# Attention, output projection and an FP8-scaled product in one kernel: the first batch's last projection tiles move into the second batch's first groups

## What is computed

```python
q = (x @ wq_w.T + wq_b).reshape(b, t, H, HD)          # H = 32, HD = 32
k = (x @ wk_w.T + wk_b).reshape(b, t, HKV, HD)        # HKV = 1
v = (x @ wv_w.T + wv_b).reshape(b, t, HKV, HD)
scores = jnp.einsum('bqhd,bkd->bhqk', q, k1) / jnp.sqrt(jnp.float32(HD))
scores = jnp.where(causal, scores, -jnp.inf)
weights = jax.nn.softmax(scores, axis=-1)
attn = jnp.einsum('bhqk,bkd->bqhd', weights, v1).reshape(b, t, H * HD)
x = _layernorm(x + attn @ wo_w.T + wo_b)
x_sim = jnp.clip(x2 * x_scale, -448, 448)             # x_scale = 448 / max|x|, over all of x
w_sim = jnp.clip(weight * w_scale, -448, 448)         # w_scale = 448 / max|weight|
x = _layernorm(x + x_sim @ w_sim * (1.0 / (x_scale * w_scale)))
```

## Time and profile before

| | |
|---|---|
| median of 3 runs | 2719.75 us (2717.81 to 2719.91) |
| the profiled execution's own time | 2719.72 us |
| its span | 2718.0 us |
| mean granted TensorE clock | 0.974 |
| PE busy | 2542.1 us, 94% of the span |
| DVE busy | 1879.0 us, 69% |
| ACT busy | 1273.5 us, 47% |
| POOL busy | 865.6 us, 32% |

### The profile page before, as it was taken

One profiled execution on the slowest core, in us unless ns is written; L12 is line 12 of the kernel. 1 busy time (PEld: TensorE's weight loads), 2 busy tenths in 40 slices (PEclk: granted clock), 3 DMA queues, 4 the chain that ended last, 5 costly groups with the idle time before them and its releaser, 6 DMA issues.

```text
span 2718.0 us, 45333 instructions
## 1 busy us (share of the span) xinstructions
PE 2542.1 (94%) x15400; PEld 1588.6 (58%) x15400; DVE 1879.0 (69%) x1432; ACT 1273.5 (47%) x1571; POOL 865.6 (32%) x569
## 2 busy tenths in 40 slices
PE   7999998889999999999878999999999997799998
PEld 5888885545544444444544555444444445688887
DVE  6343336668788889999555788888899993444444
ACT  2222224545566666777334565666777670100000
POOL 2321302433322222212334333222221223566663
PEclk9999998989999999999888999999999998899999
DMA  7343334411211111011233122111101104122221
GB/s 232 124 145 141 116 128 141 122 40 51 62 45 39 39 40 40 12 39 40 67 95 94 44 66 51 40 39 39 40 29 37 39 1 162 48 85 90 88 93 62
DMA packets 75076, 197.24 MB, mean 73 GB/s; under 512 B 8559, under 2 KB 8559, under 8 KB 72815
## 3 DMA queue, kind: packets, MB, share of 16 engines
q1 hardware_dynamic: 50220, 140.52, 17.9%
q10 hardware_dynamic: 24768, 55.59, 5.3%
HBM read 123.72 MB, written 72.35 MB: 72 GB/s over the span
## 4 chain that ended last, share of the span: by engine, by line
PE 62%; issue 7%; DVE 5%; ACT 5%; POOL 3%; DMA 1%; ACTq 1%; SPq 0%; DVEq 0%; POOLq 0%
PE bank L1165 16%; PE bank L1177 15%; PE bank L1153 13%; PE bank L1261 13%; ACT prob L689 4%; DVE acc L940 3%; PE bank L1195 2%; POOL prob L546 2%; PE bank L1187 2%; DMA q_st<-max_d 1%; PE bank L1250 1%; DVE acc L937 1%; POOL att_lo L538 0%; ACT att_hi L700 0%; DVE r_den L901 0%
## 5 line engine op out<-in xcount | busy, mean ns | idle before, releaser
L689 ACT ACTIVATE prob<-bank 128x1024 f32<-128x1024 f32 (+3 forms) x1280 | 1077.4, 897 | 627.6 <-PE bank L1165 595.2
L940 DVE TENSOR_TENSOR acc<-acc,prob 128x2048 f32<-128x2048 f32 (+3 forms) x512 | 1093.4, 2136 | 131.1 <-POOL prob L546 85.8
L1165 PE MATMUL bank<-q_st,keys 98*128 98x512 f32 (+3 forms) x2560 | 712.5, 392 | 88.6 <-ACT prob L689 63.0
L1165 PEld LDWEIGHTS bank<-q_st,keys 98*128 98x128 f32 x2560 | 427.6, 192 | 391.6 <-ACT prob L689 308.3
L1177 PE MATMUL bank<-prob,v_t 128*32 128x512 f32 (+3 forms) x5120 | 596.6, 548 | 11.1 <-POOL prob L546 11.1
L546 POOL TENSOR_SCALAR_AFFINE_SELECT prob<-prob 128x512 f32<-128x512 f32 x256 | 300.8, 1179 | 873.0 <-ACT prob L689 872.4
L1075 PE MATMUL bank<-xt_hi,w_hi 128*128 128x512 f32 x576 | 227.3, 395 | 16.4 <-DVE xt_lo L777 15.7
L1075 PE MATMUL bank<-xt_hi,w_lo 128*128 128x512 f32 x576 | 226.6, 393 | 0.0
L1075 PE MATMUL bank<-xt_lo,w_hi 128*128 128x512 f32 x576 | 226.2, 393 | 0.0
L1177 PEld LDWEIGHTS bank<-prob,v_t 128*32 128x32 f32 x5120 | 107.9, 109 | 197.8 <-issue 141.4
L1261 PE MATMUL bank<-wf_hi,xs_hi 128*128 128x512 f32 x512 | 202.8, 396 | 0.0
(11 more groups left out here) (118 smaller groups left out, 2668.7 us busy)
## 6 DMA issues: line engine op xcount, KB each, us to landing
q_st<-q_hi_d SPq DMA_DIRECT2D x128, 256.0 KB
xt_raw<-x_t SPq DMA_DIRECT2D x16, 1024.0 KB, 6.9
q_hi_d<-part_hi ACTq DMA_DIRECT2D x64, 256.0 KB, 2.1
q_lo_d<-part_lo ACTq DMA_DIRECT2D x64, 256.0 KB, 2.3
q_st<-q_lo_d SPq DMA_DIRECT2D x64, 256.0 KB
x<-x_d SPq DMA_DIRECT2D x32, 512.0 KB, 3.2
out<-y ACTq DMA_DIRECT2D x32, 512.0 KB, 2.6
res<-x SPq DMA_DIRECT2D x24, 512.0 KB, 4.0
```

The source lines that it names most:

```text
L689: nc.scalar.activation(prob[:, t % SLOTS, 2 * p:2 * p + 2, off:NB], bank[:, 2 * p:2 * p + 2, off:NB], ACT.Exp, scale=SCALE).then_inc(p_don ...
L940: nc.vector.tensor_tensor(acc[:, r, :, off:NB], acc[:, r, :, off:NB], new, ALU.add).then_inc(acc_done, 1)
L1165: last = nc.tensor.matmul(bank[:, h, off:NB], keys[:, b * JB + t // QT, t % QT * P:(t % QT + 1) * P], q_st[:, slot, h, off:NB], start=True ...
```

## The change

- The first batch's end stage is gone. Its four tiles are projected in the four pairs of j = 0 of the second batch, through `res`, `att_hi` and `att_lo` like all others. `split_place` puts ACT's cut, `fillers` PE's matmuls and `residual_places` DVE's sums: in the first of these pairs both halves of 24 matmuls stand in r = 1 (steps 1 and 3), in the other three the first half stands in steps 2 and 3 of r = 0 and the second in steps 1 and 2 of r = 1.
- Since `res` is then taken, all eight weight pieces go through the first batch's four pairs of j = 0, one in each group.
- The second batch's first scores are issued in the last step of the first batch; ACT no longer waits between the batches. The batches are written out one after the other on ACT, DVE and POOL.
- For j > 0 the second half's fillers change steps: j = 1 has 4 parts of 6 matmuls in steps 3 to 6 (before: 3 of 8 in 4 to 6), j = 2 has 6 parts in steps 3 to 8 (before 4 to 9), j = 3 has 10 parts in steps 3 to 12 (before 8 in 4 to 11). DVE's second `add_residual` with the moments stays in step 7 for j = 1 and 10 for j = 2, and moves from step 12 to 14 for j = 3.

```diff
+        def has_tile(b, j):
+            return j > 0 or b > 0
+        def split_place(j, first):
+            if j > 0:
+                return 0, key_tiles(j) // 2 - 1
+            return (0, 3) if first else (0, 0)
+        def fillers(b, j, first):
+            n = key_tiles(j)
+            if j > 0:
+                halves = [(0, t) for t in range(n // 2 + 1, n)], [(1, t) for t in range(3, n - 1 if j == 1 else n - 3)]
+            elif first:
+                halves = [(1, 1)], [(1, 3)]
+            else:
+                halves = [(0, 2), (0, 3)], [(1, 1), (1, 2)]
+        def residual_places(j, first):
+            n = key_tiles(j)
+            if j > 0:
+                return (1, 1), (1, n - 1 if j == 1 else n - 2)
+            return (1, 2 if first else 0), (1, 3)
-        def projection_steps(j, r):
-            half = key_tiles(j) // 2
-            return range(half + 1, 2 * half) if r == 0 else range(4, min(half + 4, 2 * half - 1))
...
-                    if j > 0:
+                    if has_tile(b, j):
                         tile = projected(b, j, gp)
-                        sp.wait_ge(x1_sent, stored_alone(b, j, gp) * 16 + 16)
+                        sp.wait_ge(x1_sent, tile * 16 + 16)
+                        sp.wait_ge(piece_sent, KT * 16 + 16)
                         sp.wait_ge(ln1, tile * LN + LN)
                         sp.dma_start(res[:], x_tiles[bass.ds(tile, 1)].rearrange("a p d -> p (a d)")).then_inc(res_in, 16)
                     for r in range(2):
+                        piece = 2 * gp + r
+                        if not has_tile(b, j):
+                            sp.wait_ge(piece_sent, piece * 16 + 16)
+                            sp.dma_start(res[:], one(w_f[:, bass.ds(piece, 1)])).then_inc(piece_in, 16)
...
-            with act.Fori(0, B) as b:
-                act.wait_ge(end_sent, b * (16 * QT) + 16 * QT)
-                act.wait_ge(ln1, b * (TT * LN) + LN)
+            for b in range(B):
...
-                pe.wait_ge(q_in, b * (SEQ_GROUPS * 64) + 64)
-                scores(b * SEQ_STEPS, 0, 0, 0)
+                if b == 0:
+                    pe.wait_ge(q_in, 64)
+                    scores(0, 0, 0, 0)
...
-                            elif not (last_pair and r == 1):
+                            elif not (b == B - 1 and last_pair and r == 1):
                                 pe.wait_ge(q_in, n * 64 + 128)
-                                scores(s0 + NT, 0, 1 - r, 0)
+                                scores(s0 + NT, 0, 1 - r, 0, b + 1 if last_pair and r == 1 else b)
```

More of the change, by code:

```diff
@@ L531, in _ @@
             pool.wait_ge(bo_in, 16)
-            with pool.Fori(0, B) as b:
+            for b in range(B):
                 def body(j, gp, first, last):
-                    if j > 0:
-                        tile = projected(b, j, gp)
+                    tile = projected(b, j, gp)
+                    if has_tile(b, j) and not (j == 0 and first):
                         wait_apart(pool, att_hi_cut, tile + 1)
@@ L547, in body @@
                                                     pattern=[[0, HG], [1, P]], channel_multiplier=-1).then_inc(masked, 1)
[L548 to L549 removed]
+                        if has_tile(b, j) and r == 0:
+                            if j == 0 and first:
+                                pool.wait_ge(att_hi_cut, tile + 1)
+                                heads = att[:, (j - 1) % 2 * G:(j - 1) % 2 * G + G, gp * P:(gp + 1) * P]
+                                nc.gpsimd.tensor_tensor(att_lo[:], heads, att_hi[:].bitcast(F32), ALU.subtract).then_inc(att_cut, 1)
+                            pool.wait_ge(res_in, tile * 16 + 16)
                             nc.gpsimd.tensor_tensor(res[:], res[:], bo[:], ALU.add).then_inc(res_ready, 1)
[L551 removed]
+                    if has_tile(b, j):
                         inverse_deviation(moments[:, 0], ln1, tile * LN + LN)
                 pairs_of_groups(pool, b, body)
[L555 to L556 removed]
+            for t in range(QT):
+                    tile = projected(B - 1, JB, t)
                     pool.wait_ge(att_hi_cut, tile + 1)
@@ L918, in largest @@
                 nc.vector.tensor_reduce(amax_x[:, bass.ds(tile, 1)], z, AX.X, ALU.max, apply_absolute_value=True).then_inc(ln1, 1)
-            with dve.Fori(0, B) as b:
+            for b in range(B):
                 def body(j, gp, first, last):
@@ L1214, in body @@
                                 weigh_values(n, s0, j, r, t)
-                            if t == 1 and not (first and r == 0):
+                            if t == 1 and not (b == 0 and first and r == 0):
                                 pe.wait_ge(acc_done, s0 + SLOTS)
                                 denominators(n - 1, 1 - r)
-                            if t == 3 and not (first and r == 0):
+                            if t == 3 and not (b == 0 and first and r == 0):
                                 spread_out(n - 1)
-                            if j > 0 and t in (window := projection_steps(j, r)):
-                                if t == window[0]:
-                                    tile = projected(b, j, gp)
+                            if (r, t) in (places := fillers(b, j, first)):
+                                half, part, parts = places[r, t]
+                                tile = projected(b, j, gp)
+                                if part == 0:
                                     pe.wait_ge(wo_cut, KT)
                                     pe.wait_ge(att_cut, tile + 1)
-                                    pe.wait_ge(y_read, tile * 2 + (r + 2))
-                                half_projection(att_hi, att_lo, r, Y_BANK, t - window[0], len(window))
+                                    pe.wait_ge(y_read, tile * 2 + (half + 2))
+                                half_projection(att_hi, att_lo, half, Y_BANK, part, parts)
                 pairs_of_groups(pe, b, body)
-                pe.wait_ge(acc_done, (b + 1) * SEQ_STEPS + SLOTS)
-                denominators(b * SEQ_GROUPS + (SEQ_GROUPS - 1), 1)
-                spread_out(b * SEQ_GROUPS + (SEQ_GROUPS - 1))
-                for t in range(QT):
-                    tile = projected(b, JB, t)
+            pe.wait_ge(acc_done, B * SEQ_STEPS + SLOTS)
+            denominators(B * SEQ_GROUPS - 1, 1)
+            spread_out(B * SEQ_GROUPS - 1)
+            for t in range(QT):
+                    tile = projected(B - 1, JB, t)
                     pe.wait_ge(att_cut, tile + 1)
```

97 lines of the change are left out of this document (42 added, 55 removed).

## The result

The changed kernel takes **2778.5 us** (median of 4 runs, 2776.2 to 2790.4), the kernel before 2718.8 in the same comparison: a ratio of 1.0225, 95% interval 1.020 to 1.025. It is slower by 60 us. The forecast was 2766 and slower; the sign is right, and the time lies in the range of 2728 to 2788, 12.5 us above the point. It lies outside the 2750 to 2775 to which the forecast itself gave a chance of 0.50, and next to rival 4 at 2780.

A forecast was written before the change was run, and what follows sets the result against it. PE bounds the long groups, the queries' DMA behind SP's queue the four-step pairs, ACT's wait the gap between the batches. +12.4 - 69.5 + 77.3 + 14.7 + 11.2 = +46.1 on 2719.7 gives 2766 us, range 2728 to 2788.

The forecast's parts named there:

- rival 4: PE restarts at a slow clock after the new waits in the four-step groups, eight times: +14, 2780 us; chance 0.13.
- The end stage: Between the batches: the first batch's separate stage goes, with ACT's wait for its stores: -69.5 us.
- The chain of the second batch's four-step pairs: Norm, store, residual load and then queries set r = 0 at 20.7 us; all four pairs together +77.3 us.
- The term of r = 1: Second half of those four-step pairs, with 36 tile matmuls on PE: 17.2 us, 19.4 in the first pair.
- The pieces: First batch's four-step groups: queries wait until a piece's store has landed, pairs of 22.3 us instead of 19.2: +12.4 us.
- j = 2: Pair ends: a filler moved from step 9 to step 3 delays DVE's last sums, 1.4 us x 8: +11.2 us.
- j = 3: Pair ends: late residual sum and moments delay the norm and PE's spread_out by 2.1 us, seven times: +14.7 us.
- j = 1: Pair ends: the residual sum waits for PE's last filler, whose end stays: 0 us.
- Rival 1: DVE's delay at pair ends is caught up within a group, not paid: +20.2, 2740 us; chance 0.20.
- Rivals 2 and 3: Four-step groups carry the tiles, 2699 us, slower only above 33.8 us a pair (0.11); near no change, 2722 us (0.06).

The follow-up runs named there:

- q_first: Changed kernel, but in the second batch's four-step pairs SP issues the queries of r = 1 ahead of the tile's store and the residual load: 2761.6 us.
- old_steps: Changed kernel with the fillers of j > 0 and the second residual sum and moments back in their former steps: 2751.3 us.
- masks_first: Changed kernel, former steps for j > 0, queries first in both batches, four pieces moved to j = 1, POOL's first masks and the norm before att_lo: 2694.0 us.
- before_steps: Kernel before with only the new filler steps for j > 0 and the late second residual sum and moments in j = 2 and j = 3: 2752.3 us.
- old_fill: Changed kernel with only the fillers of j > 0 back in their former steps, residual sum and moments still late: 2772.3 us.

## Why the prediction was right, and where it was off

- **The end stage: right.** The pause is gone, its PE work is back in the pairs.
- **The chain of the second batch's four-step pairs: right in mechanism.** r = 0 is 0.5 to 0.7 us longer in the regular pairs, 17.9 for 17.3 in the first and 25.9 for 25.8 in the second. **The term of r = 1 was mis-sized:** 17.2 is the time at full clock (17.0 measured with queries first). The changed kernel has 24.0 in the first pair (19.4) and 19.7 to 19.8 in the others, 12 us in sum. In the others it is the clock, 2.7 to 2.9 us each over the 17.0. The first pair's 4.6 us aren't divided by a run; in q_first, where no wait stands ahead of it, it takes 20.4. With r = 0 these are the stage's 14 us. The clock was rival 4, with 14 us and a chance of 0.13; it belonged in the sum, since the row with the slow clock behind a wait, was at hand.
- **The pieces: the size was off by 0 to 4 us** (+12.0 and +16.0 in two executions for +12.4), and the reason given was incomplete, so that the good number is partly luck. The wait for the landing is there, but taking it away changes nothing; the queue's order costs.
- **j = 2: right,** 1.4 us a pair. **j = 3: the wait was right** (2.08 for 2.1), the loss is 3.3 to 3.9: 1.3 us or more of slow clock that the step left out. The term had seven pair ends. Six show the wait, 21.0 us for 12.6; at the seventh, in the second batch's first group, PE doesn't wait for the reciprocal, and its 2.1 us were counted twice, since the 17.3 us of that group's chain hold the same shift.
- **j = 1: 0 forecast,** 0.8 and 1.5 measured by the copies, each in the block's first group. The moved fillers aren't the cause: with the steps of before the second batch has 2.9 there in old_steps and 1.5 in masks_first.
- Rival 1 (DVE's delay isn't paid) is refuted by old_steps and before_steps. Rivals 2 and 3 are refuted by pairs of 41 us, with 33.8 as the point.
- The account exceeds the forecast by 25 us in the profiled execution, the median only by 12.5: the other executions of that comparison were 11 to 14 us shorter. Which stretch they saved is not in a trace, and stays open. The profiled one, 2790.4 us, lies above the range's upper end; that the median lies inside it owes something to those shorter executions.

## What to carry to other kernels

A queue that waits for its loads to land is a serial resource: put the transfer that PE waits for next ahead of all that only has to be done some time, and look at that order before adding buffers or moving stages. Work that is moved out of a stage of its own into short groups needs a new order on every engine that it meets there (SP's queries, POOL's masks), else its chains cost more than the stage did. And where rows show a slow clock behind PE's waits, a forecast wait has to be charged with it, by a range from nothing to the price seen (here 1.3 to 2.8 us a wait), since it doesn't come each time.

## What the runs showed of the hardware

- PE waits of 2.1 us in j = 3 and 2.8 us in the four-step pairs of the changed kernel were followed by 4 us with a granted clock of 0.64 and 0.50; waits of 2.09 us in j = 3 of q_first and 2.88 us in the four-step pairs of old_fill were not (1.00). A wait of 1.45 us in j = 2 was followed by 1.00, one of 1.46 in before_steps by 0.71. The price was 1.3 us at a wait of 2.08 and 2.8 us at one of 2.84. The Trainium skill, "TensorE: Matmul & The Clock Gate", in its section on the clock's oscillation, describes short stretches of work between DMA waits that restart at the lower clock each time; the trace agrees for the changed kernel's second batch, where each of the four waits for the queries is followed by 0.50, with 2.07 us for four matmuls that take 1.09 at full clock, and not for old_fill.
- A DVE norm with one SBUF input is held by POOL's subtraction as fully as the sum of the earlier trace rows: 2.82 us for 0.81.
- A 512 KB store and a 512 KB load issued just ahead of 768 KB of queries made these take 8.8 us instead of 7.0.
